# Feed-forward of a graph transformer on one core: first products of chunk c+1 ahead of the second products of chunk c

## The reference, cut to what matters

```python
for l in range(L):                        # L = 2
    ...
    x = _batchnorm(x + attn, g1[l], beta1[l])
    ff = jax.nn.relu(x @ W1[l].T + b1[l]) @ W2[l].T + b2[l]   # 512 -> 128 -> 512
    x = _batchnorm(x + ff, g2[l], beta2[l])
```

## Time and profile before

| what | us |
|---|---|
| median of 3 runs | 3087.56 |
| lowest and highest run | 3073.77 and 3089.63 |
| span of the profiled execution | 3095.6 |
| feed-forward of layer 0 (1467.90 to 1524.84) | 56.94 |
| feed-forward of layer 1 (2593.90 to 2650.92) | 57.02 |

### The profile page before, as it was taken

One profiled execution on the slowest core, in us unless ns is written; L12 is line 12 of the kernel. 1 busy time (PEld: TensorE's weight loads), 2 busy tenths in 40 slices (PEclk: granted clock), 3 DMA queues, 4 the chain that ended last, 5 costly groups with the idle time before them and its releaser, 6 DMA issues.

```text
span 3095.6 us, 78344 instructions
## 1 busy us (share of the span) xinstructions
PE 2657.9 (86%) x32605; PEld 2143.5 (69%) x32605; DVE 1629.2 (53%) x3272; ACT 1321.1 (43%) x3690; POOL 1115.8 (36%) x1130
## 2 busy tenths in 40 slices
PE   5999997999999999758899788888888678599998
PEld 4877885777777777546488577777777465477777
DVE  5236785555555555456512355555554645656553
ACT  3324443555555555422232255555555322333432
POOL 0000002666666666400001267777777111222110
PEclk8999998999999999979999899999999889799998
DMA  5642003988899998641024489999999431122211
GB/s 195 228 175 107 31 28 140 317 313 316 309 331 322 317 325 297 222 121 41 14 97 154 160 321 354 352 349 347 350 347 352 126 113 57 38 89 92 69 59 58
DMA packets 231795, 621.75 MB, mean 201 GB/s; under 512 B 39008, under 2 KB 45792, under 8 KB 231427
## 3 DMA queue, kind: packets, MB, share of 16 engines
q0 software_dynamic: 137088, 466.78, 42.2%
q1 hardware_dynamic: 94339, 149.78, 14.6%
HBM read 538.80 MB, written 103.39 MB: 207 GB/s over the span
## 4 chain that ended last, share of the span: by engine, by line
PE 60%; DMA 16%; DVE 8%; POOL 7%; issue 6%; ACT 2%; SPq 0%; DVEq 0%; POOLq 0%; ACTq 0%
PE ps L1179 6%; DMA Y<-KVd,srcE 5%; PE ps L574 5%; PE ps L575 4%; PE ps L576 4%; DMA aggd<-stage,segs 4%; PE ps L1222 4%; PE ps L1209 4%; PE ps L774 3%; POOL Y L1096 3%; PE ps L942 2%; PE ps L944 2%; PE ps L943 2%; PE ps L1186 2%; PE ps L1872 2%
## 5 line engine op out<-in xcount | busy, mean ns | idle before, releaser
L1096 POOL DMA_INDIRECT Y<-KVd,srcE x449 | 430.2, 958 | 230.6 <-issue 115.8
L1370 ACT ACTIVATE stage<-ps,stage 128x128 f32<-128x128 f32 x832 | 294.8, 366 | 115.3 <-PE ps L1186 112.4
L1096 POOL DMA_INDIRECT WA<-KVd,srcE x186 | 179.3, 964 | 361.8 <-PE ps L576 268.1
L1351 ACT ACTIVATE work<-ps 128x512 f32<-128x512 f32 x309 | 179.8, 597 | 303.8 <-PE ps L1179 303.5
L1179 PE MATMUL ps<-ident,Y 128*128 128x128 f32 x1796 | 252.2, 280 | 32.2 <-DMA Y<-KVd,srcE 26.8
L1351 ACT ACTIVATE G<-ps 128x512 f32<-128x512 f32 x315 | 181.8, 597 | 223.5 <-PE ps L1179 223.1
L1277 DVE COPY G<-ps 128x512 f32<-128x512 f32 x208 | 143.8, 691 | 245.8 <-PE ps L1186 243.0
L574 PE MATMUL ps<-Wh,xs 128*128 128x512 f32 x600 | 238.7, 398 | 31.2 <-DVE xs L514 31.2
L1179 PEld LDWEIGHTS ps<-ident,Y 128*128 128x128 f32 x1796 | 199.2, 143 | 70.5 <-issue 49.3
L575 PE MATMUL ps<-Wl,xs 128*128 128x512 f32 x600 | 236.9, 395 | 0.0
L576 PE MATMUL ps<-Wh,xs 128*128 128x512 f32 x600 | 236.5, 394 | 0.0
(11 more groups left out here) (383 smaller groups left out, 6775.2 us busy)
## 6 DMA issues: line engine op xcount, KB each, us to landing
KVd<-stage SPq DMA_DIRECT2D x96, 256.0 KB, 2.0
aggd<-work SPq DMA_DIRECT2D x6, 2048.0 KB, 7.4
Qd<-stage SPq DMA_DIRECT2D x48, 256.0 KB, 2.0
G<-aggd SPq DMA_DIRECT2D x48, 256.0 KB, 2.7
Y<-KVd,srcE POOLq DMA_INDIRECT x449
Y<-in_x SPq DMA_DIRECT2D x4, 1536.0 KB, 14.7
G<-mixq SPq DMA_DIRECT2D x24, 256.0 KB
mixd<-rowsb SPq DMA_DIRECT2D x24, 256.0 KB
```

The source lines that it names most:

```text
L1096: pool.indirect_dma_start(out=kvs[a], out_offset=None, in_=KVd[l][:, :], in_offset=bass.IndirectOffsetOnAxis(ap=srcE[:, n:n + 1], axis=0)) ...
L1351: act.activation(kT[n % len(kT)], banks(l)[place_of(l, "k", n) % len(banks(l))][:, :], ACT.Copy).then_inc(out_a, 1)
L1370: last = act.activation(pT[g % len(pT)][:, P * i:P * (i + 1)], SC[g % 2][:, P * i:P * (i + 1)], ACT.Exp, bias=smin[:, t:t + 1], scale=-1.0 ...
```

## The change

PE's row in the feed-forward is written in another order, with another use of banks. The first product of a chunk is now a function `hidden(c)`, which writes to `PS[4]` for even and `PS[5]` for odd chunks. `hidden(0)` runs first; then, for each chunk c, `hidden(c + 1)` stands ahead of the four second products of chunk c, which use `PS[0]` to `PS[3]`, one for each f. `hidden(c)` waits for `is_normal` of chunk c and, from c = 2, for the Relu of chunk c - 2, the reader of its bank. A second product waits for the Relu of its chunk and for the addition of chunk c - 1 that reads its bank. On ACT and DVE only the bank that is read changes. `finish_pe` is the same function for both layers, so both change.

```diff
--- before.py
+++ after.py
@@ -1844,6 +1844,9 @@
             e.wait_ge(nrm, NCK * stage_no + c + 1)
             e.wait_ge(nrm_a, NCK * stage_no + c + 1)
 
+        def hidden_bank(c):
+            return PS[4 + c % 2]
+
         def finish_pe(l):
             pe.wait_ge(wa_in, WA_IN[l])
             pe.wait_ge(w_lo, WO_CUT[l] + 4)
@@ -1875,26 +1878,26 @@
                     mm.then_inc(wo_mm, 1)
                     if c + 1 < NCK and f < len(NODE_TILES[c + 1]):
                         turn_row(NODE_TILES[c + 1][f])
+            def hidden(c):
+                c0, cn = CHUNKS[c]
+                is_normal(pe, 2 * l, c)
+                if c >= 2:
+                    pe.wait_ge(relu, NCK * l + c - 1)
+                for k in range(4):
+                    mm = pe.matmul(hidden_bank(c)[:, 0:cn], W1[:, k, :], xT[:, k, c0:c0 + cn], start=(k == 0), stop=(k == 3))
+                mm.then_inc(w1_mm, 1)
+
+            hidden(0)
+            pe.wait_ge(wo_add, WO * (l + 1))
             for c, (c0, cn) in enumerate(CHUNKS):
-                for i in range(5):
-                    e = 5 * c + i
-                    bank, o = PS[e % 4], e - 4
-                    if o < 0:
-                        pe.wait_ge(wo_add, WO * (l + 1))
-                    elif o % 5 == 0:
-                        pe.wait_ge(relu, NCK * l + o // 5 + 1)
-                    else:
-                        pe.wait_ge(ff_add, WO * l + 4 * (o // 5) + o % 5)
-                    if i == 0:
-                        is_normal(pe, 2 * l, c)
-                        for k in range(4):
-                            mm = pe.matmul(bank[:, 0:cn], W1[:, k, :], xT[:, k, c0:c0 + cn], start=(k == 0), stop=(k == 3))
-                        mm.then_inc(w1_mm, 1)
-                    else:
-                        if i == 1:
-                            pe.wait_ge(relu, NCK * l + c + 1)
-                        pe.matmul(bank[:, 0:cn], W2[:, (i - 1) * P:i * P], work[:, c % 3, 0:cn], start=True, stop=True
-                                  ).then_inc(w2_mm, 1)
+                if c + 1 < NCK:
+                    hidden(c + 1)
+                pe.wait_ge(relu, NCK * l + c + 1)
+                for f in range(4):
+                    if c:
+                        pe.wait_ge(ff_add, WO * l + 4 * (c - 1) + f + 1)
+                    pe.matmul(PS[f][:, 0:cn], W2[:, f * P:(f + 1) * P], work[:, c % 3, 0:cn], start=True, stop=True
+                              ).then_inc(w2_mm, 1)
 
         def finish_act(l, meanwhile, beside_ff):
             for c, (c0, cn) in enumerate(CHUNKS):
@@ -1924,7 +1927,7 @@
                 act.wait_ge(w1_mm, NCK * l + c + 1)
                 if c >= 3:
                     act.wait_ge(w2_mm, WO * l + 4 * (c - 2))
-                act.activation(work[:, c % 3, 0:cn], PS[5 * c % 4][:, 0:cn], ACT.Relu, bias=vec[:, C_B1 + l:C_B1 + l + 1]
+                act.activation(work[:, c % 3, 0:cn], hidden_bank(c)[:, 0:cn], ACT.Relu, bias=vec[:, C_B1 + l:C_B1 + l + 1]
                                ).then_inc(relu, 1)
                 beside_ff(c)
             act.wait_ge(ln_var, LN_FIN + 2 * l + 2)
@@ -1995,7 +1998,7 @@
                     dve.wait_ge(w2_mm, i)
                     if f == 2:
                         is_normal(dve, 2 * l, c)
-                    dve.scalar_tensor_tensor(out=xT[:, f, c0:c0 + cn], in0=PS[(5 * c + f + 1) % 4][:, 0:cn],
+                    dve.scalar_tensor_tensor(out=xT[:, f, c0:c0 + cn], in0=PS[f][:, 0:cn],
                                              scalar=vec[:, C_B2 + 4 * l + f:C_B2 + 4 * l + f + 1],
                                              in1=xT[:, f, c0:c0 + cn], op0=ALU.add, op1=ALU.add).then_inc(ff_add, 1)
                     dve.wait_ge(ff_add, i)
```

## The result

The changed kernel is slower: median 3134.07 us (3128.74 to 3144.31, 6 runs) against 3079.72 us (3067.88 to 3089.63, 6 runs) of the kernel before beside it, ratio 1.0177 with a 95% interval of 1.0154 to 1.0200. That is 54 us; the sum of the prediction was 52.6. The forecast of 3140 was made on the first three runs of before, whose median was 3087.56; on 3079.72 the same sum gives 3132.3. So the 6 us between 3140 and 3134 come from that base and not from the change.

A forecast was written before the change was run, and what follows sets the result against it. PE bound the feed-forward, 7.98 us a period including the Relu wait, with DVE next. A new PE-DVE ring (31.6 us) plus the lower clock (21) added 52.6 to 3087.6, giving 3140 us, range 3112 to 3151.

The forecast's parts named there:

- the sum of the prediction: Both feed-forwards: 31.6 us for ring and ends at full clock plus 21 us for the lower clock, 52.6 us in all.
- The forecast of 3140: Whole kernel: median before of 3087.6 plus 52.6 us gives 3140 us, +1.7%; this case had chance 0.76.
- What was late next: Without the Relu wait, PE's first products of chunk c+2 wait for DVE's normalising behind chunk c's additions, about 4.1 us.
- the smaller signs: Profile after: period 13 to 14 us, first products 5.5 to 6.2, DVE idle about 4 to 7 ahead of first additions.
- The ring's length: Serial ring through PE and DVE in the feed-forward: 11.25 us a period in place of 7.98, +3.27, four periods a layer.
- Ring and ends together: Feed-forward at full clock: 2.6 + 13.1 + 0.3 - 0.2 = 15.8 us longer a layer, 31.6 for both.
- The clock: PE's clock falls in each wait: first products of chunks 2 to 5 +9.2, last full chunk +1.3 a layer; both layers +21.
- The rule cited from the Trainium skill: In products coming in bursts between waits, the clock falls in each wait and every burst starts cold; carries the 21 us.
- The ends: Feed-forward's start +2.6 us, start of chunk 5 +0.3, end -0.2, low clock at the last full chunk +1.3, per layer.
- The rival of no new wait: PE runs products without gaps, 6.90 us a period, DVE keeps up: -6.0 us for both layers, 3082, chance 0.05.
- Its other way: On PE, second products of chunk c+1 pass the waiting first products of chunk c+2; part of the rival with chance 0.05.
- The prediction's sentence that POOL changes nothing on DVE in layer 1: Layer 1's feed-forward has the same period as layer 0; POOL's work there leaves DVE unchanged, so both layers together lose 31.6.

The follow-up runs named there:

- the first and fourth experiments: Changed kernel with chunk c+2 normalised ahead of chunk c's additions: ratio 0.9965 to the kernel before; instead behind two of the four additions 1.0001, behind one 0.9990.
- the run with the clock held: Changed kernel plus four unused products into an unused bank on PE ahead of the first products of chunks 2 to 6: ratio 1.0088 to the kernel before.

## Why the prediction was right, step by step

**What was late next.** The step that decided the sign was to ask, when the Relu's wait goes, what the moved instruction itself waits for. The rows after name DVE's normalising ahead of the first products of chunks 2 to 5, idle 4.04 us where 4.1 was forecast, and of chunk 6, and the first and fourth experiments show that the place of this one step on DVE makes the loss, and in the measure that its end comes after the end of the second products: behind four additions +53.7 us by the stages, behind two +4.3, ahead of them -8.6. Of the smaller signs two were a little off: in layer 0 the first products of chunks 2 to 5 took 5.40 to 6.41 us and not 5.5 to 6.2, and DVE was idle for up to 7.36 us ahead of the first addition of chunks 1 to 4, not 7.

**The ring's length.** 11.25 us by the prediction, 11.17 in the run with the clock held. The hand-over from DVE to PE was taken as 0.14 us and is 0.04 in the chain. Ring and ends together: 31.6 forecast, 31.2 measured.

**The clock.** 21 us forecast, 22.6 measured. The first products after a wait took 5.40, 6.41, 6.30 and 6.24 us in layer 0, against 3.70 with the clock held. The forecast's 5.80 to 6.13 was taken from the start of the stage; the first burst was cheaper, because the clock was still full when the wait ended (1.00 in the wait, 0.67 behind it), the others dearer (0.84 in the wait and 0.56 behind it for the second). Against 3.70 the four lost 1.70, 2.71, 2.60 and 2.54 us, 9.55 together where 9.2 was forecast: the two misses nearly cancel, and that much of the agreement is luck. The rule cited from the Trainium skill, page "TensorE: Matmul & The Clock Gate", section "HAM oscillation — how this bites in real kernels", is borne out in its price: each of the four bursts above was slower than with the clock held, and the two for which the stretch is shown ran at mean clocks of 0.67 and 0.56. The cold start at every burst is not borne out for the first one, which began at the full clock (1.00 in its first 1.05 us) and slowed only after that.

**The ends.** The start of the stage cost 2.5 us (the second products of chunk 0 start 9.13 us after the first products, 6.67 before; forecast 2.6). The short chunk and the end cost 2.2 us a layer by the rows in layer 0 (0.9 to the start of chunk 5, 1.3 from there); the forecast had 0.3 - 0.2 + 1.3 = 1.4. It took the low clock's cost once, and it falls on both: on the first products of chunk 6 (1.95 us where 0.99 stood in the earlier trace rows) and on the second products of chunk 5.

**The rival of no new wait** was priced too low: six us for both layers. The kernel that realises it saves 8.6 by the stages, since PE needs only 4.26 us a period at chunk 6, not the 6.90 the rival took; of these 2.6 us a layer DVE's 5.53 us of additions to chunk 4 take 1.3 back. Its sign and its size within 0.5% were right. Its other way, a second product passing the waiting first product, did not come about in the changed kernel: the Relu of chunk 1 started at 1476.24 and took 0.69 us, and the second products of chunk 1 started at 1488.91, behind the first products of chunk 2.

## What to carry to other kernels

When an instruction is moved ahead of a wait on one engine, look at what feeds it on the other engines: that work must be done by the time the moved instruction has its turn, or a wait that was hidden by a period of slack can become a ring with no overlap. Here one step on DVE, moved with it, turns a loss of 1.8% into a gain of 0.35%. And on PE a wait has two prices, its own length and the slower products behind it; in this ring the second was 22.6 of 53.7 us.

## What the runs showed of the hardware

DVE's normalising, a tensor-by-scalar operation from SBUF to SBUF, took 2.00 us for two instructions beside POOL's subtractions and 0.99 without them, and 5.68 us for four, in place of 1.92, beside a longer row of them; it ended 0.28 and 0.29 us after POOL's row did (2606.77 against 2606.49, 2646.82 against 2646.53). DVE's additions, which read one operand from PSUM, were not slowed: in the kernel before, those at 2619.65 and 2621.04 took 0.75 and 0.73 us beside POOL's subtractions of 2619.02 to 2621.53. The Trainium skill, page "SBUF — State Buffer", section "Who interferes with whom", states that these two engines share a pair of ports, and that when DVE works in a mode that uses two ports, which the page lists as possible for `tensor_scalar`, the one that issues first holds the pair for its whole instruction and the other blocks. The runs agree with the blocking, in that DVE both times came to its end right behind POOL; in which mode DVE worked, no run here shows.

The prediction's sentence that POOL changes nothing on DVE in layer 1 holds for the kernel before and the changed one, where normalising took 0.99 us, but only because POOL's subtractions and the normalising happened not to fall together in time.
